# A gated attention and expert block on one core: scale columns multiplied one by one, weight high parts moved ahead, and the router's product turned round

## What is computed

```python
def block(x, ctx, g_xattn, g_ffn, Wq, Wk, Wv, Wo, bo, gate_w, expert_w, expert_b):
    h = layernorm(x)
    q, k, v = heads(h @ Wq), heads(ctx @ Wk), heads(ctx @ Wv)
    a = softmax(q @ k.T / 8) @ v
    x = x + tanh(g_xattn) * (merge(a) @ Wo + bo)
    xt = layernorm(x).reshape(-1, 256)
    probs = softmax(xt @ gate_w.T)              # router, 8 experts
    w, sel = top_k(probs, 2)
    y = sum(w_e * (xt @ expert_w[e].T + expert_b[e]) for e in sel)
    return x + tanh(g_ffn) * y
```

## Time and profile before

| | |
|---|---|
| median of 3 runs | 975.36 us (972.61 to 977.74) |
| profiled execution | 974.66 us, its span 972.9 us |
| mean granted TensorE clock | 0.980 of full speed |
| PE / DVE busy | 918.1 us (94%) / 865.2 us (89%) |
| ACT / POOL busy | 743.4 us (76%) / 648.1 us (67%) |

### The profile page before, as it was taken

How to read it: one execution, slowest core, us unless ns; L and a number is a source line. 1 busy time by engine, 2 the same in 40 slices (tenths; PEclk the granted TensorE clock), 3 DMA queues, 4 the chain that set the end, 5 groups by cost and what they waited for, 6 DMA issues and landing times.

```text
span 972.9 us, 28780 instructions
## 1 busy us (share of the span) xinstructions
PE 918.1 (94%) x11336; PEld 616.0 (63%) x11336; DVE 865.2 (89%) x1845; ACT 743.4 (76%) x1093; POOL 648.1 (67%) x450
## 2 busy tenths in 40 slices
PE   6588799999999999999999999999999999999997
PEld 4145455677657775577656776577765776676773
DVE  6799899998998989899898989989898998999767
ACT  3898999688984879758895789958797588978610
POOL 3877778576784867668684777948677586867400
PEclk9999999999999999999998999999998999999999
DMA  7499799888997889868897789979899578988900
GB/s 245 114 197 163 121 184 180 146 158 156 182 193 110 158 143 196 177 126 162 160 188 137 146 167 167 182 135 164 146 192 174 121 157 171 173 157 166 148 23 23
DMA packets 549142, 150.97 MB, mean 155 GB/s; under 512 B 537592, under 2 KB 547216, under 8 KB 548752
## 3 DMA queue, kind: packets, MB, share of 16 engines
q1 hardware_dynamic: 549008, 149.13, 80.9%
HBM read 11.70 MB, written 4.19 MB: 16 GB/s over the span
## 4 chain that ended last, share of the span: by engine, by line
PE 58%; DVE 26%; ACT 8%; issue 7%; DMA 1%; POOL 0%; SPq 0%; ACTq 0%; DVEq 0%
PE MB L1343 30%; PE PV L1516 11%; PE ST L1494 11%; DVE nmax L1026 9%; ACT p_s L850 3%; ACT pf L840 3%; PE MB L1355 3%; DVE v_s L1017 2%; DVE QL L1006 2%; DVE o_n L1049 2%; DVE KL L1006 1%; PE ST L1343 1%; DVE stats L884 1%; PE MB L1435 1%; DVE shifts L1032 1%
## 5 line engine op out<-in xcount | busy, mean ns | idle before, releaser
L662 POOL TENSOR_TENSOR p_s<-pf,p_s 128x1024 f16<-128x1024 f32 x254 | 542.2, 2137 | 241.0 <-ACT p_s L850 190.8
L840 ACT ACTIVATE pf<-ST,shifts 128x512 f32<-128x512 f32 x512 | 323.7, 691 | 93.6 <-DVE shifts L1032 92.7
L1026 DVE TENSOR_REDUCE nmax<-ST 128x2 f32<-128x1024 f32 x256 | 310.0, 1215 | 25.9 <-PE ST L1494 24.4
L850 ACT ACTIVATE p_s<-pf 128x1024 f16<-128x1024 f32 x254 | 270.5, 1068 | 3.2
L1516 PEld LDWEIGHTS PV<-v_s,pt_s 128*128 128x128 f16 x6096 | 208.9, 99 | 41.8 <-issue 24.8
L1516 PE MATMUL PV<-v_s,pt_s 128*128 128x65 f16 x6096 | 220.3, 195 | 3.1 <-DVE o_n L1049 3.0
L1343 PE MATMUL MB<-ex_s,x2t_s 128*128 128x256 f16 (+1 forms) x1380 | 166.0, 275 | 0.1
L1343 PEld LDWEIGHTS MB<-ex_s,x2t_s 128*128 128x128 f16 x1380 | 132.0, 98 | 21.5 <-issue 1.3
L1494 PE MATMUL ST<-KH,QH 64*128 64x512 f16 x512 | 100.8, 390 | 13.4 <-ACT pf L840 10.2
L1343 PE MATMUL MB<-xt_s,wq_s 128*128 128x512 f16 x384 | 95.6, 386 | 4.4 <-DVE v_s L1017 1.6
L981 DVE SCALAR_TENSOR_TENSOR acc<-MB,m,acc 128x256 f32<-128x256 f32 x224 | 95.5, 475 | 4.3 <-PE MB L1343 3.6
(11 more groups left out here) (177 smaller groups left out, 1018.6 us busy)
## 6 DMA issues: line engine op xcount, KB each, us to landing
pt_s<-p_s SPq DMA_TRANSPOSE x508, 2.8
xin<-x SPq DMA_DIRECT2D x7, 512.0 KB, 4.7
out<-acc SPq DMA_DIRECT2D x7, 512.0 KB, 3.7
kvin<-kv_t SPq DMA_DIRECT2D x8, 256.0 KB, 4.1
stage_e<-expert_t SPq DMA_DIRECT2D x1, 2048.0 KB, 10.9
stage_o<-wo SPq DMA_DIRECT2D x1, 1024.0 KB, 6.5
stage_q<-wq SPq DMA_DIRECT2D x1, 768.0 KB, 6.4
xin<-x SPq DMA_DIRECT2D x2, 256.0 KB, 2.7
```

The lines of the kernel that those rows point to most:

```text
L662: pool.tensor_tensor(p_s[:, slot, 1, :, :], pf[:, it.ring(p, u, PF_SLOTS), :, :], p_s[:, slot, 0, :, :], ALU.subtract).then_inc(p_lo, 1)
L840: last = act.activation(pf[:, (n - 1) % PF_SLOTS, i, :], ST[u % 2][:, i, :], ACT.Exp, bias=shifts[:, u % 2, i:i + 1])
L850: act.activation(p_s[:, it.ring(p, u, P_SLOTS), 0, :, :], pf[:, it.ring(p, u, PF_SLOTS), :, :], ACT.Copy).then_inc(p_hi, 1)
L1026: dve.tensor_reduce(nmax[:, t % 2, :, 0], ST[t % 2][:, :, :], AX.X, ALU.max, negate=True)\
```

## The change

Three parts.

1. The job `router`, its `take` and the matrix `fold` go. The job `logits` now holds a 128 x 128 block of `x2t_s` as the stationary operand and streams the 16 columns of `gt_s`: 4 blocks of tokens, 2 parts, 2 halves of the channels, so 16 matmuls, one job, with the tokens on partitions. DVE adds the two parts of each logit by one more `tensor_reduce`, within the PSUM bank, and waits for it. The factor `g_back` moves into ACT's exponential.
2. `v_mul` is written by two one-column `tensor_scalar` in place of one `scalar_tensor_tensor` over two columns, and `o_mul` and `s_val` are made by `tensor_scalar` with the second factor as a per-partition scalar, in place of `tensor_tensor`.
3. In the prologue the high parts of `wk` rest and `wv` move on ACT ahead of the high part of q0. The counts that POOL and DVE wait for follow. The dummy matmuls change: 10 in place of 5 ahead of `bound`, 3 ahead of q0 in place of 2 ahead of k0, and in the epilogue 6 ahead of `logits` in place of 5 and 3.

```diff
 PE_ORDER LOOP
-        "scores x2t1 q5 bound values values router", "scores ot1 v2,1 logits values values k4", "scores",
+        "scores x2t1 q5 bound values values", "scores ot1 v2,1 logits values values k4", "scores",
 PE_ORDER LAST
-        "scores router ot1 k5", "scores logits wo0,0 wo0,1 q5", "scores",
+        "scores ot1 k5", "scores logits wo0,0 wo0,1 q5", "scores", ...
 DVE_ORDER LOOP
-        "maximum take shift take take normalise take", "maximum shift take normalise take take",
+        "maximum take shift take take normalise take", "maximum shift take normalise take",
 DVE_ORDER LAST
-        "maximum take take normalise shift take take", "maximum take take take shift take",
+        "maximum take take normalise shift take take", "maximum take take shift take", ...
-BUSY_PRO = {("xt", 0): 15, ("bound",): 5, ("k", 0): 2}
-BUSY_EPI = {NEXT_X2T: 14, ("router",): 5, ("logits",): 3}
+BUSY_PRO = {("xt", 0): 15, ("bound",): 10, ("q", 0): 3}
+BUSY_EPI = {NEXT_X2T: 14, ("logits",): 6}
...
-            pool.tensor_tensor(fold[:, :], ident[0:2 * EXPERTS, 0:EXPERTS], ident[0:2 * EXPERTS, EXPERTS:2 * EXPERTS],
-                               ALU.add).then_inc(const_pool, 1)
...
-                pool.wait_ge(w_hi, 4 + n)
+                pool.wait_ge(w_hi, 3 + n)
...
                     act.activation(wk_s[:, 0, early], stage_k[:, early], ACT.Copy, scale=w_mul[:, 1:2])\
                        .then_inc(w_hi, 1)
+                    act.activation(wk_s[:, 0, rest], stage_k[:, rest], ACT.Copy, scale=w_mul[:, 1:2])\
+                       .then_inc(w_hi, 1)
+                    act.activation(wv_s[:, 0, :], stage_v[:, :], ACT.Copy, scale=w_mul[:, 0:1]).then_inc(w_hi, 1)
                 if name == ("k", 0):
                     act.activation(wq_s[:, 0, :, rest], stage_q[:, :, rest], ACT.Copy, scale=q_mul[:, 0:1])\
                        .then_inc(w_hi, 1)
-                    act.activation(wk_s[:, 0, rest], stage_k[:, rest], ACT.Copy, scale=w_mul[:, 1:2])\
-                       .then_inc(w_hi, 1)
...
                     elif part == "ph":
-                        act.activation(wv_s[:, 0, :], stage_v[:, :], ACT.Copy, scale=w_mul[:, 0:1]).then_inc(w_hi, 1)
...
-                act.activation(prob[:, :, :], logit[:, :, :], ACT.Exp).then_inc(lg_exp, 1)
+                act.wait_ge(late_scale, 1)
+                act.activation(prob[:, :, :], logit[:, :, :], ACT.Exp, scale=g_back[:, 0:1]).then_inc(lg_exp, 1)
...
-                elif kind == "router":
-                    last = dve.tensor_scalar(logit_parts, m[0:2 * EXPERTS, :], g_back[0:2 * EXPERTS, 0:1], None, ALU.mult)
...
-                    raw = m[:, 0:TT * EXPERTS].rearrange("p (t e) -> p t e", t=TT)
+                    parts_ = m[:, 0:2 * TT * EXPERTS].rearrange("p (t a e) -> p t e a", t=TT, a=2)
+                    raw = m[:, 2 * TT * EXPERTS:3 * TT * EXPERTS].rearrange("p (t e) -> p t e", t=TT)
+                    dve.tensor_reduce(raw, parts_, AX.X, ALU.add).then_inc(lg_sum, 1)
+                    dve.wait_ge(lg_sum, it.b)
...
-                        dve.scalar_tensor_tensor(v_mul[:, of % 2, :], w_div[:, :], c_div[:, 0:1], v_rec[:, :],
-                                                 ALU.mult, ALU.mult)
+                        for n in range(2):
+                            dve.tensor_scalar(v_mul[:, of % 2, n:n + 1], v_rec[:, n:n + 1], w_div[:, n:n + 1],
+                                              c_div[:, 0:1], ALU.mult, ALU.mult)
...
-                        dve.tensor_tensor(s_val[:, :], v_div[:, 1:2], q_back[:, :], ALU.mult).then_inc(scale_done, 1)
+                        dve.tensor_scalar(s_val[:, :], v_div[:, 1:2], q_back[:, 0:1], None, ALU.mult).then_inc(scale_done, 1)
...
-                dve.tensor_tensor(o_mul[:, b % 2:b % 2 + 1], v_div[:, 0:1], o_back[:, :], ALU.mult)
+                dve.tensor_scalar(o_mul[:, b % 2:b % 2 + 1], v_div[:, 0:1], o_back[:, 0:1], None, ALU.mult)
...
-                dve.wait_ge(w_hi, 3)
+                dve.wait_ge(w_hi, 5)
...
-                elif kind in ("router", "logits"):
-                    if kind == "router":
-                        pe.wait_ge(job_hi, it.last_done(HI, ("x2t", 0), ("x2t", 1)))
-                    else:
-                        pe.wait_ge(job_free, it.done(JOBS, ("router",)) + BANKS)
-                    if kind == "logits":
-                        pe.wait_ge(const_pool, CONST_POOL)
+                elif kind == "logits":
+                    pe.wait_ge(job_hi, it.last_done(HI, ("x2t", 0), ("x2t", 1)))
+                    pe.wait_ge(job_free, it.last_done(JOBS, ("x2t", 0), ("x2t", 1)) + BANKS)
...
                 elif kind == "logits":
                     for t in range(TT):
-                        last = pe.matmul(m[:, t * EXPERTS:(t + 1) * EXPERTS], logit_parts[:, tile(t)],
-                                         fold[:, :], start=True, stop=True)
+                        for a in range(2):
+                            for c in range(LC):
+                                last = pe.matmul(m[:, t * 2 * EXPERTS:(t + 1) * 2 * EXPERTS], x2t_s[:, a, c, tile(t)],
+                                                 gt_s[:, c, :, :].rearrange("p a e -> p (a e)"),
+                                                 start=(a == 0 and c == 0), stop=(a == 1 and c == LC - 1))
```

More of the change, by code:

```diff
@@ L94 @@
         "scores k4 values values v1,1", "scores", "scores q4 values q3 values", "scores x2t0 x2t1 v0,1 values values ot0",
-        "scores router ot1 k5", "scores logits wo0,0 wo0,1 q5", "scores",
[L96 to L100, removed]
+        "scores ot1 k5", "scores logits wo0,0 wo0,1 q5", "scores", "scores values v2,1 values pair1,4 values values",
+        "scores", "scores pair0,4 values pair1,2 pair0,3 values k6", "scores", "scores q6 values pair0,6 v3,1", "scores",
+        "scores pair1,0 values k7 ot2", "scores pair0,5 ot3 values pair1,1 values", "scores",
+        "scores gates pair1,7 wo1,1 wo1,0", "scores", "scores values values q7", "scores values values",
+        "scores bias0 ot4 values values", "scores bias1 values pair0,7", "scores",
         "scores ot5 pair1,5 pair0,0 wo2,0 pair1,6 pair0,1 wo2,1 pair0,2 pair1,3 values",
@@ L162 @@
         "maximum normalise shift take", "maximum take take shift take normalise",
-        "maximum take take normalise shift take take", "maximum take take take shift take",
[L164 to L169, removed]
+        "maximum take take normalise shift take take", "maximum take take shift take", "maximum shift take route1 take",
+        "maximum shift", "maximum normalise take shift route2 take normalise", "maximum route3 take shift take",
+        "maximum shift take normalise take", "maximum shift take", "maximum shift take take", "maximum",
+        "maximum shift take shift take normalise take take", "maximum shift take take take", "maximum shift",
+        "maximum take take shift normalise take take", "maximum shift", "maximum normalise shift take",
+        "maximum shift normalise", "maximum shift take normalise", "maximum shift take take take", "maximum shift",
         "maximum shift take take take take take take normalise take take take",
@@ L228 @@
 LAST_EXPERTS = [("expert", t, e) for t in range(TT) for e in range(EC)]
-LAST_JOBS = ([("x2t", 0), ("x2t", 1), ("router",), ("logits",)] + LAST_EXPERTS[:TT] + [("gates",)] + LAST_EXPERTS[TT:-3]
+LAST_JOBS = ([("x2t", 0), ("x2t", 1), ("logits",)] + LAST_EXPERTS[:TT] + [("gates",)] + LAST_EXPERTS[TT:-3]
              + [("bias", 0), ("bias", 1)] + LAST_EXPERTS[-3:])
@@ L1424, in produce @@
                     last = turned(m, lambda t: xn[:, t, name[1] * P:(name[1] + 1) * P], TT if it.kind == EPI else None)
-                elif kind == "router":
-                    for a in range(2):
-                        if a == 1:
-                            pe.wait_ge(job_free, it.last_done(JOBS, ("x2t", 0), ("x2t", 1)) + BANKS)
-                        for c in range(LC):
-                            last = pe.matmul(m[0:2 * EXPERTS, :], gt_s[:, c, :, :].rearrange("p a e -> p (a e)"),
-                                             x2t_s[:, a, c, :], start=(a == 0 and c == 0),
-                                             stop=(a == 1 and c == LC - 1))
                 elif kind == "logits":
                     for t in range(TT):
-                        last = pe.matmul(m[:, t * EXPERTS:(t + 1) * EXPERTS], logit_parts[:, tile(t)],
-                                         fold[:, :], start=True, stop=True)
+                        for a in range(2):
[3 more added lines that the diff above has]
+                                                 start=(a == 0 and c == 0), stop=(a == 1 and c == LC - 1))
                 elif kind == "gates":
```

9 lines of the change are left out of this document (3 added, 6 removed).

## The result

| | median | lowest to highest | runs |
|---|---|---|---|
| before | 975.84 us | 972.61 to 977.74 | 4 |
| after | 946.62 us | 944.65 to 948.67 | 4 |

The ratio is 0.9704, with a 95% interval from 0.9671 to 0.9738: 3.0% faster. The forecast was 940 us, with a range of 932 to 954 us. Of the profiled executions, that of before took 974.66 us (span 972.9) and that of after 948.67 us (span 946.9).

A forecast was written before the change was run, and what follows sets the result against it. PE and DVE were taken to hand the pace to each other, with DVE stalling on POOL in each middle batch. 16.2 + 12.5 + 1.4 + 1.5 + 4.0 = 35.6 us off 974.7 gave 939.1, stated as 940 us; range 932 to 954.

The forecast's parts named there:

- LOOP, six batches: Batches 1 to 6: PE no longer waits for DVE's scaling and DVE's stall goes, 2.7 us each, 16.2 us.
- clock in the loops: Behind the stall in loop batches: without PE's idle time its clock holds, as in batch 1, 12.5 us.
- LAST: Last batch: the chain runs through both router jobs, which become 16 matmuls of 0.5 us, saving 1.4 us.
- epilogue: Epilogue: the logits' maximum comes earlier behind the low part of x2t, 944.15 in place of 945.67, 1.5 us.
- prologue: Prologue: earlier high parts on ACT remove PE's wait for POOL's low part of wv; 4.0 us, bounds 2 and 5.5.
- The place and the mechanism: Line 994 in batches 1 to 6: v_mul ends with POOL's instruction after 2.15 us, PE waits, and its clock often falls.
- batch 1 as control: Loop batch with the same stall but its clock kept, period 112.0 us: 3.1 us more PE speed shortens the period equally.
- rival C: Loop batches: DVE and ACT take the pace, so half of the 16.2 us is lost, 948 us; chance 0.12.
- The upper bound for the 16 new matmuls: New logits on PE: 2.0 us if each matmul costs as much as one float32 one (0.98 / 8); 0.5 expected.
- A: Loop batches: the one-column scalings wait for POOL as well, leaving 1.0 us gain per batch, 950 us; chance 0.17.
- D: Six batches: each of the four one-column instructions waits for a p_s of its own, slower, 988 us; chance 0.02.
- B: Loop batches: the clock still falls in the same five places, the 16-column matmuls being light, 952 us; chance 0.08.

The follow-up runs named there:

- e8: The kernel after, unchanged, timed again on the same chip: 945.86 us, ratio 0.9677.
- e1: The kernel before with part 2 alone (one-column scalings), the old router kept: 956.62 us, ratio 0.9785.
- e2: The kernel before with part 1 alone (new logits), v_mul still one two-column instruction: 955.74 us, ratio 0.9772.
- e3: The kernel after with part 3 undone, so parts 1 and 2 only: 950.32 us, ratio 0.9716.
- e6: The kernel after with one more two-column tensor_scalar, into a scratch tile, behind the v_mul pair: 951.02 us, ratio 0.9735.
- e7: The kernel after with o_mul and s_val back as one-column tensor_tensor (two SBUF inputs): 951.18 us, ratio 0.9730.
- e5: The kernel before with 14 dummy 128-column matmuls meant to fill PE's wait before the fold; they ran behind it: 984.31 us, ratio 1.0081.
- e11: e2 with four light 8-column float32 dummy matmuls (eight records) behind PE's wait, ahead of k4: 970.52 us, ratio 0.9927.
- e12: e2 with four dense 128-column float32 dummy matmuls (eight records) behind PE's wait, ahead of k4: 962.89 us, ratio 0.9845.
- e10: The kernel after with batch 0's ACT and DVE orders changed, late_div in three one-column instructions, four fewer epilogue dummies: 940.02 us, ratio 0.9615.
- e9: e2 with eight light 8-column float32 dummy matmuls (sixteen records) behind PE's wait, ahead of k4: 981.00 us, ratio 1.0016.

## Why the prediction was right, and where its sizes were off

The forecast was 35.4 us less than the median before; 29.2 us less was measured. The profiled executions of before (974.66 us) and of e8 (945.86 us) differ by 28.8 us. By marks in the two traces, lead being how much earlier the same maximum starts, it splits so beside the terms of the forecast:

| term | forecast | measured | how |
|---|---|---|---|
| LOOP, six batches | 16.2 | 13.7 | 6 x 2.28 (111.97 less 109.69) |
| clock in the loops | 12.5 | 12.5 | 9.5 in five periods (3.14, 1.61, 3.14, 1.60), 3.0 behind the sixth |
| LAST | 1.4 | 0.55 | lead of e8 over before, 27.41 to 27.96 |
| epilogue | 1.5 | 0.8 | 28.8 less the lead of 27.96 |
| prologue | 4.0 | 4.0 | 82.35 less 78.35, means of 8 and 6 profiles |
| not forecast | 0 | -2.8 | start of e8 0.8 later, batch 0 0.8 longer, periods of e8 1.2 longer |

**The place and the mechanism were right.** The stall is DVE waiting for POOL, one column of `tensor_scalar` escapes (12 of 12 beside POOL), PE's wait goes, and with it the falls of the clock. That the clock's term agrees to the tenth of a microsecond is no check, since forecast and table take it from the same uneven periods of before. The check is that five periods of after are equal to 0.02 us at clock 1.00. Taking batch 1 as control was the step that found 12.5 us in which no instruction goes away.

**LOOP was sized 0.4 us too high a batch.** The forecast took PE's 2.9 us, less 0.2 for ACT, and DVE's 2.7. DVE's count was the weak one. I had allowed 0.15 us for the added instruction. In the trace the `v_mul` pair takes 0.46, and `o_mul` and `s_val` cost 0.05 more each with a scalar operand. From `v_mul` to the end of `s_val` the kernel after needs 0.70 us, before 2.29 (400.08 to 402.37): 1.59, and 0.74 for the scaling. That is 2.33 by durations, and 2.27 from the start of `v_mul` to that of the next maximum (3.00 less 0.73); the period moved by 2.28. In e1 that stretch fell by 1.59 us, from 2.99 to 1.40, and the period by 1.59. So these two look as if DVE sets the pace and PE's further head start is worth nothing, as rival C said in kind. It isn't the whole rule: in e2 the stretch fell by 0.66 and the period by 1.19.

**LAST was 0.9 too high.** The two router jobs were taken off a chain that then had ACT just behind it. The trace of after has PE standing 0.80 us for the exponential between the job ahead of them and the logits, where in before it went on without a wait (855.75):

```profile
830.92 0.39 PE L1480 MATMUL ST<-KH,QH 64*128 64x512 f16 x2 [0.80 <-ACT pf L832]
```

The forecast's 1.4 less this 0.80 is 0.6, near the 0.55 measured. A saving on the engine of the chain ends where the next engine is.

**The epilogue was 0.7 too high in e8, and not elsewhere.** In after and e8 the clock fell there, the twelve records of the six dummies before the logits ran at 0.22 and 0.21 us each, and the logits came 0.9 and 0.7 us past their input. In e3, e6 and e7, with the same dummies at the full clock, the maximum starts 0.95 us behind the input, against 1.06 in the forecast, and the epilogue is 1.9 us shorter than in before. The term left out that the clock could fall there; why it did in two of these five isn't known.

**The prologue was right in size and in its steps.** Counted from the prologue's `v_mul`, v0,0 comes 3.4 us earlier with part 3 (13.5 us, mean of the six profiles, against 17.0 in the eight), where 3.2 was forecast. Its six matmuls, 2.74 us in all eight, take 1.47 in five of the six, as forecast; the profile of after, with 2.09, is the odd one. POOL did collide with `wq`'s low part, 2.45 us, as forecast.

**One bound was misread.** The price of the float32 matmuls was taken as 0.98 us over eight, but the eight are records of four instructions, 0.245 us each. The upper bound for the 16 new matmuls would then have been 3.9 us, not 2.0. They took 0.55, so nothing came of it.

**The rivals.** A's world was built in e6: one stall of the same length in the same place, part 1 and 3 in. A said 950; e6 measured 951.0. It didn't come, since one column doesn't wait. D needed that too. B would have needed a wait together with light matmuls; the 16-column logits have no wait before them. What the forecast had as the cause, that PE stood and then did a microsecond of 8-column matmuls, was the pair that e1, e2, e5, e11 and e12 take apart; it said so without knowing that both are needed.

## What to carry to other kernels

If a tiny DVE instruction ends with POOL's, give it one column and scalar operands: it leaves POOL's way and costs 0.20 to 0.27 us in place of 0.15. Do so for every such instruction behind it as well, or the wait moves to the next (e7, e10). Where the same work takes different times in different rounds, take the undisturbed round as control and look for a wait followed by narrow matmuls; two edits that each remove the pair don't add up. A gain of a few microseconds in the part with the input transfers wants intervals between two marks, over several profiles, since one pair of traces misled here.

## What the runs showed of the hardware that was not expected

- 1.6 to 1.8 us of standing cost no clock before dense matmuls (e2, e5, e12: 1.00), though 3.6 us in batch 0 did (0.50 behind it in before and after, 1.00 in e10 without that wait), nor did a microsecond of 8-column matmuls right behind work (e1: 1.00). Together they cost 1.6 or 3.1 us (before, e11), changing from batch to batch in the same code.
- An instruction of one column with two SBUF tensors waits for POOL's end as one of three columns does: 1.78 us (e7; `late_div` 1.78), 2.10 us (e10's `o_back`). In the `tensor_scalar` form the border lies between one column (0.27 us) and two (1.79 us).
- A `tensor_scalar` of one column takes 0.20 us with one tensor operand as its scalar and 0.27 with two, against 0.15 with constants (e10's `late_div`) and 0.15 for the one-column `tensor_tensor` when POOL is idle.
- A float32 matmul appears as two records (e5: 14 instructions, 28 records; e11: 4 and 8): what the prediction calls eight small matmuls are four instructions. e9 doubled the dose for not knowing it.
- The packets of the queue that carries inputs, outputs and the turned probabilities took 94.7% of the span of 16 DMA engines after and 80.9% before, with the same 549008 packets and 149.13 MB. It is 80 to 83% in all four profiles with the old router and 90 to 96% in nine of the ten with the new one (84% in e6). Why stays open.
